# Two mixture-of-experts layers on one core: which all-token passes multiply by plain fp32 slabs

## What is computed

```python
logits = xf @ w_router.T                 # 128 x 8; the two best experts of each token
routed += c[:, e] * (silu(xf @ Wg[e].T) * (xf @ Wu[e].T)) @ Wd[e].T   # for each expert e
out = routed + swiglu(xf, sg, su, sd)    # L1 alone has this shared expert
```

## Time and profile before

| what | value |
|---|---|
| median of 3 runs | 1235.61 us (1233.38 to 1236.67) |
| the profiled execution, its own time | 1238.13 us |
| its span in the profile | 1236.4 us |
| granted TensorE clock, mean | 0.988 |
| busy: TensorE matmul / VectorE / ScalarE | 94% / 46% / 36% |
| L1's mixture, from its first product to its last slab | about 287 to 571 us |
| L3's mixture, likewise | about 701 to 1223 us |

### The profile page before, as it was taken

The page is one execution under the profiler, slowest core; times in us unless marked ns, Lnnn a source line. Parts: engine busy times, 40 slices in busy tenths (PEclk is TensorE's granted clock), DMA queues, the critical chain, the costliest instruction groups (busy, mean ns, idle before and its releaser), DMA issues.

```text
span 1236.4 us, 15668 instructions
## 1 busy us (share of the span) xinstructions
PE 1157.1 (94%) x6393; PEld 731.4 (59%) x6393; DVE 568.8 (46%) x868; ACT 440.8 (36%) x494; POOL 22.0 (2%) x47
## 2 busy tenths in 40 slices
PE   5999999889999999987899999999999999888996
PEld 4676786667855355534766776565665555444642
DVE  6977642437644234201656675464554533333310
ACT  4765512224633233100434354343444422223200
POOL 2000000000000000000000000000000000000000
PEclk9999999999999999999999999999999999899999
DMA  9988646944999999999357498999999999999994
GB/s 374 423 363 342 232 174 215 417 160 195 389 418 424 426 424 426 426 424 426 144 212 267 173 404 308 427 426 424 426 425 426 425 425 425 426 425 425 426 426 199
DMA packets 42630, 443.13 MB, mean 358 GB/s; under 512 B 4784, under 2 KB 4944, under 8 KB 8000
## 3 DMA queue, kind: packets, MB, share of 16 engines
q1 hardware_dynamic: 39744, 427.05, 83.5%
q0 software_dynamic: 2816, 15.09, 3.2%
HBM read 441.73 MB, written 0.39 MB: 358 GB/s over the span
## 4 chain that ended last, share of the span: by engine, by line
PE 72%; DMA 17%; DVE 7%; ACT 3%; issue 1%; POOL 0%; SPq 0%; DVEq 0%; ACTq 0%
PE PJ L1839 15%; DMA scratch<-in_weights 11%; PE PJ L1811 10%; PE AC L1876 8%; PE TP L1898 6%; DMA extra<-in_weights 5%; PE PJ L1820 5%; PE AC L1635 3%; PE AC L1647 3%; PE MS L1489 2%; PE PJ L1802 2%; PE TP L1849 1%; PE PJ L1595 1%; DMA ring<-in_weights 1%; PE PJ L1548 1%
## 5 line engine op out<-in xcount | busy, mean ns | idle before, releaser
L1839 PE MATMUL PJ<-scratch,picked 128*64 128x512 f32 (+1 forms) x564 | 146.2, 601 | 3.7 <-DMA scratch<-in_weights 3.7
L1898 PE MATMUL TP<-ring,extra 128*64 128x512 f32 (+3 forms) x752 | 123.5, 488 | 8.1 <-issue 4.0
L1254 DVE SCALAR_TENSOR_TENSOR act<-low,CB,PJ 128x512 f32<-128x512 f32 x51 | 38.0, 746 | 171.4 <-PE PJ L1839 87.8
L1272 DVE TENSOR_TENSOR ring_lo<-ring,w_hi_u 128x1536 fp32r<-128x1536 f32 x46 | 79.6, 1756 | 68.5 <-ACT w_hi_u L845 68.4
L828 ACT ACTIVATE low<-PJ 128x512 f32<-128x512 f32 x51 | 30.2, 592 | 220.5 <-PE PJ L1839 148.0
L1839 PE MATMUL PJ<-ring,picked 128*32 128x512 f32 (+1 forms) x456 | 101.6, 594 | 0.4 <-DMA ring<-in_weights 0.4
L1898 PEld LDWEIGHTS TP<-ring,extra 128*64 128x64 f32 (+1 forms) x752 | 49.6, 126 | 70.0 <-issue 61.9
L845 ACT ACTIVATE w_hi_u<-ring 128x1536 fp32r<-128x1536 f32 x46 | 66.9, 1483 | 55.6 <-PE AC L1876 24.9
L1272 DVE TENSOR_TENSOR ring_lo<-ring,w_lo_u 128x1536 fp32r<-128x1536 f32 x40 | 68.9, 1755 | 37.7 <-ACT w_lo_u L845 37.7
L1839 PEld LDWEIGHTS PJ<-scratch,picked 128*64 128x64 f32 (+1 forms) x564 | 42.7, 126 | 60.3 <-issue 59.6
L1820 PE MATMUL PJ<-ring_lo,XTh 128*128 128x512 f32 x198 | 77.9, 394 | 0.0
(11 more groups left out here) (437 smaller groups left out, 2086.9 us busy)
## 6 DMA issues: line engine op xcount, KB each, us to landing
ring<-in_weights SPq DMA_DIRECT2D x164, 1536.0 KB, 18.7
scratch<-in_weights SPq DMA_DIRECT2D x80, 1536.0 KB, 21.9
extra<-in_weights SPq DMA_DIRECT2D x25, 1536.0 KB, 21.9
extra<-in_attn POOLq DMA_DIRECT2D x11, 768.0 KB, 9.8
extra<-in_attn POOLq DMA_DIRECT2D x6, 512.0 KB, 9.6
scratch<-in_weights SPq DMA_DIRECT2D x4, 768.0 KB, 25.2
scratch<-in_ffn_vectors POOLq DMA_DIRECT2D x1, 2688.5 KB, 12.4
extra<-in_x SPq DMA_DIRECT2D x1, 384.0 KB, 3.0
```

Of the source, the lines that this page charges most:

```text
L1254: v.scalar_tensor_tensor(hexp, silu, weight, PJ[:, SEG:2 * SEG], ALU.mult, ALU.mult) \
L1272: v.tensor_tensor(slab_lo(n)[:, half * HALF:(half + 1) * HALF], half_slab(n, half), hi_half(n, half).bitcast(F32), ALU.subtract).then_inc( ...
L1839: ins = mm(dst[c], x[:, t, c], slab_at(LOAD[q, kind, side])[:, t * SEG:(t + 1) * SEG], start=(t == 0), stop=(t == KT - 1))
L1898: ins = mm(Y[c, a:b], hT_of(q)[:, t * P:(t + 1) * P][:, c], slab_at(LOAD[q, "d", side])[:, t * D + a:t * D + b], start=(j == j0 and t == 0 ...
```

## The change

Pass 1 in L1 and pass 19 in L3 become plain like pass 0 and 18. The copies and subtractions that stood ahead of the router and around it are now those of pass first+2, `tokens_lo` goes behind u(first+1), and "apart" is g of pass first+2. In pass first+1 ScalarE and VectorE no longer split g and u of the next pass, since these are already done. Slots, the order of slabs and the order on TensorE stay as they are.

```diff
-PLAIN = [MOE[l]["first"] for l in (1, 3)]
+PLAIN = [MOE[l]["first"] + i for l in (1, 3) for i in range(2)]
...
-                whole_hi(first + 1, "g")
+                whole_hi(first + 2, "g")
                 transposed(k)
...
-                whole_hi(first + 1, "u", (0,))
+                whole_hi(first + 2, "u", (0,))
...
-                whole_hi(first + 1, "u", (1,))
+                whole_hi(first + 2, "u", (1,))
...
-                    if q > first:
+                    if q > first + 1:
                         whole_hi(q + 1, "g")
                         whole_hi(q + 1, "u")
...
-                    dve.wait_ge(S("pe_u"), first + 1)
+                    dve.wait_ge(S("pe_u"), first + 2)
...
-                whole_lo(first + 1, "g")
+                whole_lo(first + 2, "g")
...
-                whole_lo(first + 1, "u")
+                whole_lo(first + 2, "u")
...
-                tokens_lo()
                 hidden(first)
...
-                    whole_lo(q + 1, "g")
+                    if q > first + 1:
+                        whole_lo(q + 1, "g")
+                    else:
+                        tokens_lo()
                     hidden(q)
-                    whole_lo(q + 1, "u")
+                    if q > first + 1:
+                        whole_lo(q + 1, "u")
...
-                    if q == first:
+                    if q in PLAIN:
                         n = LOAD[q, kind, 0]
...
-                        apart = q == first + 1 and kind == "g"
+                        apart = q == first + 2 and kind == "g"
...
-                    if q == first:
+                    if q in PLAIN:
                         n = LOAD[q, "d", 0]
```

## The result

The changed kernel takes 1240.39 us in the median of 8 runs (1238.86 to 1244.31), against 1235.26 us of the kernel before in the same comparison (8 runs, 1232.09 to 1236.78). The ratio is 1.0050, with a 95% interval from 1.0036 to 1.0063: 6.2 us slower, between 4.4 and 7.8, or 5.1 us by the medians. The forecast was 1241.7 us, 6.1 us slower.

The account below looks back on a forecast made before the run. TensorE bounds each mixture's first part, the weight stream its second. TensorE's delay at the heads, 3.1 us in L1 plus 3.0 in L3, makes 6.1 us on the 1235.6 us median: 1241.7 us, range 1236.5 to 1245.5.

Parts of the forecast that it names:

- The bound, and where the loss enters: Each mixture is bound first by TensorE, then by the slab stream; delay enters at the head, where DMA runs dry.
- Lost time isn't made up: Behind slab 54 in L1, likewise in L3: all releases 3.1 us late, the full DMA engines never catching up.
- TensorE's price of the pass: Plain g, u and d in pass first+1 make TensorE later by 3.1 us in L1 and 3.0 in L3.
- ScalarE and VectorE at nothing: The copies, subtractions and remainder each mixture loses gain 0 us, since TensorE did not wait for them.
- The moves ahead of the router: Splits of pass first+2 ahead of the router, same in number and size: 0 us, +2 us kept for a late slab.
- The stream: Slab 54 (L1) and slab 147 (L3) go out late with nothing ahead: 3.1 and 3.0 us reach the end.
- Slab 147 stands likewise: In L3, slab 147 and some before it pass on TensorE's delay as slab 54 does in L1; 3.0 us.
- The sum of the range: From 1236.5 us (absorbed in one mixture, with spread) to 1245.5 (both upper ends, about 8.4 us, and 1.5 spread).
- The signs: Expected profile: 5.2 us products, slab 54 issued near 332.6, DMA share about 0.85, last slabs 3 and 6 us later.
- A: The stream absorbs the delay: 1238.7 us if in one mixture (chance 0.08), 1235.6 us if in both (0.05).
- B: ScalarE's chain of copies, not TensorE, held the slots at the heads, so dry time comes back: 1227.5 us; chance 0.04.
- C: The slow start also strikes slab 54, or fp32 costs the four passes: 1244 us and up; chance 0.04.

Follow-up runs that it names:

- e3: Kernel before with pass 10 (L1) and pass 31 (L3) also plain, where TensorE is the bound but the queue is deep: ratio 1.0006 (0.9992 to 1.0020).
- e4: Kernel before with passes 45 and 47 of L3 also plain, where TensorE waits for slabs: ratio 1.0003 (0.9992 to 1.0013).
- e1: The change in L1's mixture alone (pass 1 plain), against the kernel before: ratio 1.0024 (1.0014 to 1.0033), 3.0 us slower.
- e2: The change in L3's mixture alone (pass 19 plain), against the kernel before: ratio 1.0040 (1.0026 to 1.0054), 3.2 to 6.7 us slower.
- e5: Kernel before, all splits kept, with 28 idle matmuls (6.25 us) behind u(first+1) in each mixture: ratio 1.0101 (1.0086 to 1.0115), 12.5 us slower.
- e9: Kernel before, all splits kept, with 14 idle matmuls (3.12 us) behind u(first+1) in each mixture: ratio 1.0057 (1.0039 to 1.0075), 7.0 us slower.
- e7: Kernel before with L1's gather 2 put ahead of d of pass 1, its copy moved earlier too: ratio 1.0019 (1.0008 to 1.0029).
- e10: Changed kernel with L3's gathers 2 to 4 moved to passes 36 and 37 and L1's gather 2 earlier: 1.0031 (1.0019 to 1.0043) against the kernel before.

## Why the prediction was right

- **The bound, and where the loss enters.** Right. The drop of the DMA share at the heads, e3 and e4 against e1 and e2, and the slope of about one in e5 show it from three sides. "Lost time isn't made up" is seen in the 405.1 to 405.5 us behind slab 159.
- **TensorE's price of the pass.** 3.1 and 3.0 us forecast, 3.0 measured for both. The rows decided well against a price of exactly four to three, which would have given 4.2 us in a mixture and 8.3 in all: measured 3.0, and 6.2 in all, at most 7.8. In these rows one plain matmul costs 0.86 us (5.15 for 6) and one of the split 0.23 (4.15 for 18), which is 3.7 to 1 and not 4 to 1; so three for one save a fifth and not a quarter.
- **ScalarE and VectorE at nothing.** Right by e9, within its some 3 us.
- **The moves ahead of the router.** Right: 291.88 with a start 0.4 us earlier. L3's slab 132 was no late one either: ScalarE begins its copy of it at 690.77, 0.55 us later than before, and the first gated slab goes out at 707.7 instead of 707.1, later by as much. `tokens_lo` behind u of pass 1 cost nothing on TensorE.
- **The stream.** In L1 right in size: slab 54 2.9 us later once the earlier start is taken off, the last slab 2.6 us later. "Slab 147 stands likewise" was right for its issue but not for its landing, which shrank from 8.7 to 6.2 us. I read "8.7" as a slow start that belongs to slab 147 and could also strike slab 54. The other traces show one draw from a spread: with the same instructions ahead, slab 147 needs 6.3 to 8.7 us. For the same reason "both slabs are at the short end" was no good reading of 8.7, and slab 54 had not "nothing ahead": slab 53 had 1.6 us to go when it was issued. The 2.3 us of the upper bound are thus scatter of the head, not a mechanism.
- **The sum of the range.** The bounds as stated, 3.1 + 2.3 us for each mixture, make 10.8 us for both, and the 2 us kept for the router would come on top. The range used 8.4 (5.4 + 3.0) and left these 2 us out. The measured 6.2 lies inside either way.
- **The signs.** Met: 5.2 us for g, u and d; the chain leaves TensorE at 486.23; slab 54 at 332.1 with 6.1 us to landing. The DMA share of 315 to 345 us fell to 0.88, not to 0.85. The last slab of L1 came 2.1 us later and that of L3 2.4, not 3 and 6: the start and the granted clock between the mixtures moved the other way by 2.0 us together, and L3's 1.9 us is within its scatter.
- **Rivals.** A fell with e1 and e2, each clear of 1. B had only 0.1 us to gain from the start, and the changed kernel shows ScalarE waiting 4.37 us for gather 2 instead. C is not seen: slab 54 landed in 6.1 us, and the pass costs 3.0 us and not 4.2.
- **What was luck.** That 6.1 and 6.2 us differ by 0.1. The interval alone is 3.4 us wide, the two mixtures alone add to 7.9 us by time (e1, e2), and the two traces show 4.5. What is supported is 3 us of TensorE's time in each mixture that reach the end about one for one, not the tenth. Adding the cost to the median and not to the single profiled execution was right, since an execution's stretch between the mixtures and its end differ from others by up to 3.3 and 1.8 us whatever the kernel.

What is still open: L3's share (e2 says 3.2 to 6.7 us for 3.0 us of TensorE), the small loss in e7, and e10's time. A relief of ScalarE and VectorE with TensorE's work unchanged was not tried, since the subtractions can't be left out without TensorE reading slabs that nobody split.

## What to carry to other kernels

Where a stream of loads is full for most of a stage, look for the few microseconds in which it is not: in this kernel TensorE's time cost about one for one there and nothing that could be told elsewhere, even where TensorE had no gap. A short time from issue to landing marked these places; move work that isn't needed yet out of them and put nothing in. That an engine is busy without a break does not by itself make its time count, if the stage ends in a wait for loads.

## What the runs showed of the hardware

- TensorE's granted clock alone moves a single profile of this kernel by some us. From 571 to 640 us it was 0.98, 0.95 or 0.93 in the 13 traces, which is about 3.4, 6.8 or 10.2 us at 1.2 GHz and the rest at 2.4; TensorE had short waits for slabs just before (busy for 76.84 of 88 us in the kernel before). The distance from L1's last slab to L3's first gated one goes with it: 134.9 us at 0.98, 136.4 to 136.6 at 0.95 and 138.0 to 138.2 at 0.93, with one exception (e9, 0.95 and 137.6). What lies behind the last slab is 12.9 to 13.0 us in the four traces in which the clock is at 1.2 GHz right behind the landing of slab 268, and 11.2 to 11.3 in the others. So differences of 3 us between two single profiles of this kernel mean nothing until their clocks are compared.
- A slab of 1536 KB lands 6.1 to 6.7 us after its issue with nothing ahead of it (slabs 45 and 136 in all 13 traces), while the full queue moves 425 GB/s, a slab in 3.7 us. With the one ahead still landing it varies: slab 147, with the same instructions ahead, took 6.3 to 8.7 us in six traces. In the slowest of them it landed some 6.6 us behind the slab before it, though issued 2.1 us ahead of that slab's landing. So the DMA engines lose time around a nearly empty queue even when it isn't quite empty.
- An fp32 matmul of 128 x 128 against 128 columns takes two records and 0.22 us (6.25 us for 28). Against 512 columns it takes 0.86 us, and an fp32r matmul of that size 0.23 us.
